# A selective state-space layer's first stage: the logarithm's table first, two casts on ScalarE, the first channels spread by 32-row products, and another order of the scan's steps

## The reference, cut to what matters

```
xn = _ln(x, ln1_g, ln1_b);  xm = _ln(xn, ln_g, ln_b)
xc = silu(conv(xm @ w1_w + w1_b))
delta = softplus(xc @ dt_w + dt_b)
Bt = xc @ Bp_w + Bp_b;  Ct = xc @ Cp_w + Cp_b
A = -exp(A_log)
for each position t:                       # h has 128 channels x 16 states
    h = exp(delta_t * A) * h + delta_t * Bt * xc_t
    y_t = sum over states of h * Ct
mo = ((y + D_p * xc) * silu(xm @ v1_w + v1_b)) @ w2_w + w2_b
x = mo + res;  ...feed-forward, residual, layernorm, next sublayer
```

## Time and profile before

| | |
|---|---|
| median of 3 runs | 486.89 us (486.88 to 487.8) |
| profiled execution | 487.24 us, of it 485.1 us span |
| busy of the span: PE, DVE, ACT, POOL | 87%, 63%, 43%, 30% |
| logarithm done on ScalarE | 24.4 us |
| first scan begins, last scan ends | 32.83 us, 63.62 us |

### The profile page before, as it was taken

One profiled execution on the slowest core, in us unless ns is written; L12 is line 12 of the kernel. 1 busy time (PEld: TensorE's weight loads), 2 busy tenths in 40 slices (PEclk: granted clock), 3 DMA queues, 4 the chain that ended last, 5 costly groups with the idle time before them and its releaser, 6 DMA issues.

```text
span 485.1 us, 7466 instructions
## 1 busy us (share of the span) xinstructions
PE 423.2 (87%) x2852; PEld 269.4 (56%) x2860; DVE 306.9 (63%) x712; ACT 206.8 (43%) x268; POOL 145.0 (30%) x138
## 2 busy tenths in 40 slices
PE   5867989999999999789999878698578999997984
PEld 5665645444555556556778355344434445556874
DVE  4789976676666665416213587953697777338754
ACT  1765623333333322153323388574154445546320
POOL 3226647877777774100302200000200000005111
PEclk9989999999999999999999887999998999999998
DMA  8611000000023110610440430000000000010000
GB/s 306 263 34 59 1 0 2 1 1 1 0 84 134 45 45 0 219 51 1 110 59 17 62 40 3 3 3 1 0 1 3 1 3 1 2 34 1 1 1 22
DMA packets 7791, 19.58 MB, mean 40 GB/s; under 512 B 1862, under 2 KB 3686, under 8 KB 7238
## 3 DMA queue, kind: packets, MB, share of 16 engines
q1 hardware_dynamic: 7756, 19.10, 13.5%
HBM read 17.26 MB, written 1.15 MB: 38 GB/s over the span
## 4 chain that ended last, share of the span: by engine, by line
PE 60%; DVE 21%; ACT 5%; issue 5%; POOL 5%; SPq 2%; DMA 1%; DVEq 0%; POOLq 0%
PE ps L1373 58%; DVE ps L1170 3%; DVE mx_a L1174 2%; POOL big L588 2%; SPq L445 1%; ACT big L768 1%; DVE big L983 1%; DVE ps L978 1%; POOL rstd L521 1%; PE ps L1385 1%; POOL big L595 1%; PE ps L1753 1%; DMA ident<-in_ident 1%; DVE big L1332 1%; DVE attn_w L917 1%
## 5 line engine op out<-in xcount | busy, mean ns | idle before, releaser
L1373 PE MATMUL ps<-big,late 128*32 128x256 f32 (+4 forms) x792 | 99.8, 383 | 11.8 <-DVE mid L909 4.5
L1373 PEld LDWEIGHTS ps<-big,late 128*32 128x32 f32 (+3 forms) x800 | 38.9, 117 | 52.0 <-issue 22.0
L794 ACT ACTIVATE big<-ps 128x1024 f32<-128x1024 f32 x48 | 48.9, 1023 | 40.3 <-PE ps L1373 39.8
L1373 PE MATMUL ps<-late,big 128*128 128x128 f32 (+1 forms) x448 | 64.1, 275 | 1.6 <-DVE mx_x L1170 1.3
L519 POOL TENSOR_SCALAR vareps<-meanvar 128x4 f32<-128x4 f32 (+2 forms) x11 | 2.6, 232 | 197.4 <-DVE meanvar L886 193.7
L732 ACT ACTIVATE big<-ps 128x1024 f32<-128x1024 f32 x32 | 32.8, 1024 | 65.3 <-PE ps L1373 58.9
L1373 PEld LDWEIGHTS ps<-late,big 128*128 128x128 f32 (+1 forms) x448 | 44.7, 152 | 25.2 <-issue 21.0
L588 POOL TENSOR_TENSOR big<-big 128x512 f32<-128x512 f32 x32 | 41.0, 1283 | 28.2 <-DVE big L1055 28.2
L1170 DVE CUSTOM_DVE_ANT_0 ps<-ps,big 128x512 f32<-128x512 f32 x64 | 42.6, 717 | 10.0 <-PE ps L1373 6.9
L1055 DVE TENSOR_SCALAR big<-big 128x1024 f32<-128x1024 f32 x32 | 27.6, 864 | 33.3 <-ACT big L732 33.3
L1373 PE MATMUL ps<-ident 128*128 128x128 f32 x232 | 30.3, 293 | 5.7 <-DMA ident<-in_ident 5.7
(11 more groups left out here) (255 smaller groups left out, 691.8 us busy)
## 6 DMA issues: line engine op xcount, KB each, us to landing
attn_w<-in_w_x SPq DMA_DIRECT2D x1, 2560.0 KB, 13.1
big<-parts_kx SPq DMA_DIRECT2D x18, 128.0 KB
late<-in_w_up SPq DMA_DIRECT2D x1, 2048.0 KB, 8.9
late<-in_w_dn SPq DMA_DIRECT2D x4, 512.0 KB, 3.9
attn_w<-in_w_up SPq DMA_DIRECT2D x1, 1024.0 KB, 5.9
attn_w<-in_w_dn SPq DMA_DIRECT2D x1, 1024.0 KB, 7.9
parts_kx<-ctx_r SPq DMA_DIRECT2D x1, 768.0 KB, 3.3
rowv<-in_rowv SPq DMA_DIRECT2D x1, 576.0 KB, 4.1
```

Source lines behind the costliest of these rows:

```text
L794: nc.scalar.activation(ex1[:, n % 3, :].rearrange("p (r n) -> p r n", r=2), ps[:, 2 * (n % 2):2 * (n % 2) + 2, :], ACT.Exp, scale=scale).t ...
L1373: return nc.tensor.matmul(o, lhsT, rhs, start=start, stop=stop, skip_group_check=shared)
```

## The change

- `nc.scalar.activation(act_table, ..., ACT.Ln, scale=-1.0)` stands behind xc's Silu, ahead of the exponentials; the one-element Exp call ahead of the loop is gone.
- delta's first and second bf16 part are made by ScalarE, the second behind `Cn`; the third part is made by VectorE instead of GpSimd. delta * xc is computed ahead of delta's remainder.
- q = 0 is not stacked: its six copies are gone. Its steps take three 32-row products per kind, straight from `dparts`, accumulating in the bank, each waiting for its own part.
- `ORDER` takes (0, 2), (1, 2) as steps 4 and 5, so q = 2 and 3 begin at step 6; the sums are called at steps 9, 11 and 14, with `SLOT` for the slots of `hC`.
- The 18 transfers are issued in the order of `QUADS`; the first eight hold the six of q = 1 and two of delta for q = 2 and 3.
- `values0(0, 0)` is no longer called at step 0; step 1 calls both `values0(0, 0)` and `values0(0, 1)`.

```diff
+        ORDER = ([(0, 0), (0, 1), (1, 0), (1, 1), (0, 2), (1, 2), (2, 0), (3, 0), (2, 1), (3, 1),
+                  (2, 2), (3, 2)] + [(q, 3) for q in range(4)])
+        SUMMED = ((0, 2, 6, 7), (1, 3, 8, 9), (4, 5, 10, 11), (12, 13, 14, 15))
+        SLOT = (0, 1, 2, 3, 4, 5, 6, 7, 0, 2, 6, 7, 1, 3, 0, 2)
+        QUADS = ([(0, 0, 1), (0, 0, 2), (0, 1, 1), (1, 0, 1), (0, 0, 3), (0, 2, 1), (1, 1, 1), (1, 2, 1)]
+                 + [(0, i, q) for q in (2, 3) for i in (1, 2)]
+                 + [(1, i, q) for q in (2, 3) for i in range(PARTS)])
...
-            pool.wait_ge(S["delta_parts"], 2)
-            nc.gpsimd.tensor_tensor(dparts[:, 0, 2, :], dtmp[:, 0, :], dparts[:, 0, 1, :], ALU.subtract
-                                    ).then_inc(S["delta_parts"], 1)
...
             nc.scalar.activation(xc[:], cv[:, 0, :], ACT.Silu).then_inc(S["xc_done"], 1)
+            nc.scalar.activation(act_table[:], neghalf[:, 0:1], ACT.Ln, scale=-1.0)
...
+            act.wait_ge(S["delta_done"], 1)
+            nc.scalar.activation(dparts[:, 0, 0, :], dl[:, 0, :], ACT.Copy).then_inc(S["delta_parts"], 1)
             nc.scalar.activation(Cn[:], ps[:, 5, :], ACT.Identity, bias=v("Cp_b")
                                  ).then_inc(S["BC_done"], 1)
+            act.wait_ge(S["delta_rest"], 1)
+            nc.scalar.activation(dparts[:, 0, 1, :], dtmp[:, 0, :], ACT.Copy
+                                 ).then_inc(S["delta_parts"], 1)
...
-            set_table(ACT.Exp)
-            act.wait_ge(S["delta_parts"], PARTS)
-            for i in range(PARTS):
-                ins = nc.scalar.activation(quads[32 * i:32 * i + 32, 0, 0, :], dparts[0:32, 0, i, :],
-                                           ACT.Copy)
-            ins.then_inc(S["delta_quads"], 1)
...
+            nc.vector.scalar_tensor_tensor(dl[:, 0, :], cv[:, 1, :], 0.0, dtmp[:, 2, :],
+                                           ALU.max, ALU.add).then_inc(S["delta_done"], 1)
...
+            dve.wait_ge(S["delta_parts"], 2)
+            dve.wait_ge(S["delta_rest"], 1)
+            nc.vector.tensor_tensor(dparts[:, 0, 2, :], dtmp[:, 0, :], dparts[:, 0, 1, :], ALU.subtract
+                                    ).then_inc(S["delta_parts"], 1)
...
-            for i in range(PARTS):
-                ins = nc.vector.tensor_copy(quads[32 * i:32 * i + 32, 1, 0, :], dparts[0:32, 1, i, :])
-            ins.then_inc(S["dx_quads"], 1)
...
+            def spread(kind, s, q, i):
+
+                bank = 2 * kind + s % 2
+                if q:
+                    return mm(ps[:, bank, :], sel_g[:, i, :], quads[:, kind, q, :])
+                for part in range(PARTS):
+                    pe.wait_ge(S[("delta_parts", "dx_parts")[kind]], part + 1)
+                    ins = mm(ps[:, bank, :], sel_g[0:32, i, :], dparts[0:32, kind, part, :],
+                             part == 0, part == PARTS - 1)
+                return ins
...
+                elif s == 6:
                     pe.wait_ge(S["late_quads"], 16 * 4 * PARTS)
...
-                if s in (7, 9, 14):
-                    y_of((7, 9, 14).index(s))
-                if s == 0:
+                if s in (9, 11, 14):
+                    y_of((9, 11, 14).index(s))
+                if s == 1:
 
                     pe.wait_ge(ld["x0"], 16)
                     pe.wait_ge(S["cxnT_done"], 2)
-                values0(s // 2, s % 2)
+                    values0(0, 0)
+                if s:
+                    values0(s // 2, s % 2)
```

More of the change, by code:

```diff
@@ L276, in program @@
             "dt_ps", "z_done", "BC_ps", "BC_done", "lg_done", "delta_parts", "dx_parts",
-            "delta_quads", "dx_quads", "second_quads", "late_quads",
+            "delta_done", "delta_rest", "second_quads", "late_quads",
             "spread_d", "spread_x", "dA_done", "dBx_done", "scan_done", "hC_done", "y_ps",
@@ L318, in own @@
             return link
-        ORDER = ([(0, 0), (0, 1), (1, 0), (1, 1), (2, 0), (3, 0), (2, 1), (3, 1)]
-                 + [(q, i) for i in (2, 3) for q in range(4)])
-        SUMMED = ((0, 2, 4, 5), (1, 3, 6, 7), (8, 9, 10, 11), (12, 13, 14, 15))
+        ORDER = ([(0, 0), (0, 1), (1, 0), (1, 1), (0, 2), (1, 2), (2, 0), (3, 0), (2, 1), (3, 1),
[5 more added lines that the diff above has]
+                 + [(1, i, q) for q in (2, 3) for i in range(PARTS)])
         KEYS = {"a": T, "x": CS}
@@ L438, in _ @@
             sp.dma_start(eb[:], a["eb"].partition_broadcast(P)).then_inc(ld["e1"], 16)
-            for q in (1, 2, 3):
-                for kind, parts in enumerate(("delta_parts", "dx_parts")):
-                    for i in range(PARTS):
[L444 to L447, removed]
+            for kind, i, q in QUADS:
+                sp.wait_ge(S["dx_parts" if kind else "delta_parts"], i + 1)
+                sp.dma_start(quads[32 * i:32 * i + 32, kind, q, :], dparts[32 * q:32 * q + 32, kind, i, :]
+                             ).then_inc(S["second_quads" if q == 1 else "late_quads"], 16)
             def spread_max(L):
@@ L541, in _ @@
                 if s >= 8:
-                    pool.wait_ge(S["y_ps"], 1 if s == 8 else 2)
-                nc.gpsimd.tensor_tensor(hC[:, s % 8, :], hs[:, s % 4, :], Cn[:],
+                    pool.wait_ge(S["y_ps"], 1 if s < 12 else 2)
+                nc.gpsimd.tensor_tensor(hC[:, SLOT[s], :], hs[:, s % 4, :], Cn[:],
                                         ALU.mult).then_inc(S["hC_done"], 1)
@@ L959, in _ @@
             dve.wait_ge(S["lg_done"], 1)
[L960 to L965, removed]
+            nc.vector.scalar_tensor_tensor(dl[:, 0, :], cv[:, 1, :], 0.0, dtmp[:, 2, :],
+                                           ALU.max, ALU.add).then_inc(S["delta_done"], 1)
+            dve.wait_ge(S["delta_done"], 1)
             dve.wait_ge(S["xc_done"], 1)
             link(nc.vector.tensor_tensor(dl[:, 1, :], dl[:, 0, :], xc[:], ALU.mult))
-            split(dl[:, 1, :], [dparts[:, 1, i, :] for i in range(3)], dtmp[:, 1, :], S["dx_parts"])
-            dve.wait_ge(S["dx_parts"], PARTS)
-            for i in range(PARTS):
-                ins = nc.vector.tensor_copy(quads[32 * i:32 * i + 32, 1, 0, :], dparts[0:32, 1, i, :])
-            ins.then_inc(S["dx_quads"], 1)
+            dve.wait_ge(S["delta_parts"], 1)
+            nc.vector.tensor_tensor(dtmp[:, 0, :], dl[:, 0, :], dparts[:, 0, 0, :], ALU.subtract
+                                    ).then_inc(S["delta_rest"], 1)
+            nc.vector.tensor_copy(dparts[:, 1, 0, :], dl[:, 1, :]).then_inc(S["dx_parts"], 1)
+            dve.wait_ge(S["dx_parts"], 1)
+            link(nc.vector.tensor_tensor(dtmp[:, 1, :], dl[:, 1, :], dparts[:, 1, 0, :], ALU.subtract))
+            dve.wait_ge(S["delta_parts"], 2)
+            dve.wait_ge(S["delta_rest"], 1)
+            nc.vector.tensor_tensor(dparts[:, 0, 2, :], dtmp[:, 0, :], dparts[:, 0, 1, :], ALU.subtract
+                                    ).then_inc(S["delta_parts"], 1)
+            nc.vector.tensor_copy(dparts[:, 1, 1, :], dtmp[:, 1, :]).then_inc(S["dx_parts"], 1)
+            dve.wait_ge(S["dx_parts"], 2)
+            nc.vector.tensor_tensor(dparts[:, 1, 2, :], dtmp[:, 1, :], dparts[:, 1, 1, :], ALU.subtract
+                                    ).then_inc(S["dx_parts"], 1)
             dve.wait_ge(S["BC_done"], 1)
@@ L1414, in _ @@
             pe.wait_ge(ld["sel"], 32)
-            pe.wait_ge(S["delta_parts"], PARTS)
             pe.wait_ge(S["gate_done"], 1)
@@ L1424, in y_of @@
                     q, i = ORDER[s]
-                    ins = mm(ps[32 * q:32 * q + 32, 4, :], sel_y[:, i, :], hC[:, s % 8, :],
+                    ins = mm(ps[32 * q:32 * q + 32, 4, :], sel_y[:, i, :], hC[:, SLOT[s], :],
                              i == 0, i == 3)
@@ L1448, in _ @@
                     pe.wait_ge(S["dA_done"], s - 1)
[L1449 to L1451 removed]
+                if s == 2:
                     pe.wait_ge(S["second_quads"], 16 * 2 * PARTS)
[L1453 removed]
+                elif s == 6:
                     pe.wait_ge(S["late_quads"], 16 * 4 * PARTS)
[L1455 to L1457 removed]
+                spread(0, s, q, i).then_inc(S["spread_d"], 1)
                 if s >= 2:
                     pe.wait_ge(S["scan_done"], s - 1)
[L1460 to L1464 removed]
+                spread(1, s, q, i).then_inc(S["spread_x"], 1)
+                if s in (9, 11, 14):
+                    y_of((9, 11, 14).index(s))
+                if s == 1:
                     pe.wait_ge(ld["x0"], 16)
                     pe.wait_ge(S["cxnT_done"], 2)
[L1468 removed]
+                    values0(0, 0)
+                if s:
+                    values0(s // 2, s % 2)
             pe.wait_ge(S["v0_done"], 2 * NPAIR)
```

## The result

The changed kernel takes 491.69 us (median of 6 runs, 489.44 to 493.07) against 487.35 (6 runs of before beside it, 486.88 to 488.24): ratio 1.0081, interval 1.0055 to 1.0107. It is slower; the forecast was 487.4, with 488.8 as the upper end. Repeated later beside 30 runs of before, it came out at 491.88, ratio 1.0055 (1.0033 to 1.0077). One execution of a later version, order_only, took 826.38 us and stands in no ratio.

What follows compares the result with a forecast made beforehand. The chain from softplus through transfers and scans bounds the kernel, VectorE pacing the loop. Terms -0.57, -0.49, +1.41, -0.75 and +0.86 gave +0.5: 487.4 us, range 486.9 to 487.9, over the cases 485.6 to 488.8.

Steps and rivals of the forecast that it cites:

- Ahead of the loop: From softplus to the first scan: added table load +1.50, shorter sequence behind it; first scan at 32.26 instead of 32.83, -0.57.
- Step 2: Eight value products partly at half clock, then the pair out at 36.7; scan 2 at 37.4 against 37.05, +0.35.
- I forecast the same fall and return: TensorE's clock ahead of scan 2 would halve at 32.0 and come back at 35.4, as in the kernel before.
- -1.05 at step 1: Scan 1 at 34.11 against 35.17 before, from -0.57 at the first scan and -0.49 more.
- the term that was put at +1.41: Step 2's share of the sum: loss from eight value products, partly at half clock, between steps 1 and 2.
- stays low longer: Rival, 22%: 32-row products delay the clock's return past about 36.1; scan 2 at 38.4 to 39.0, time 488.4 to 489.
- Step 4: No transfer left to wait for; scan 4 at 41.1 against 41.50, a term of -0.75.
- Step 12: Six products instead of two where TensorE is the limit, nothing hiding them: +0.86, scan 12 at 57.36.
- held-clock rival: Five short products in the gap keep the clock full; scan 2 at 35.96, -0.9, 486.0 us; chance 30%.
- So the effect on the time is the shift of the last scan: Nothing behind the loop absorbs a shift, so the total moves as the last scan does: 62.90 against 62.40.

Runs made afterwards that it cites:

- order_only: Kernel before with only the new order of steps, sums and transfers; stacks, casts and loads unchanged: ratio 0.9998 to before.
- no_ln: Changed kernel without the added one-element logarithm call: median 487.97 us, ratio 1.0001 to before.
- before_ln: Kernel before with only the added one-element logarithm call: ratio 1.0028 to before.
- stack12: Changed kernel with step 12 alone multiplied by two 96-row products, of parts stacked by six more transfers: 491.32 us, ratio 1.0043 to before.
- gap_full: Changed kernel with seven idle 128-row products between delta's three 32-row products: median 489.53 us, ratio 1.0024 to before.
- Combined: Changed kernel without the added call, step 12 stacked, three and two idle 128-row products, value products four and four: 487.10 us, ratio 0.9963 to before.
- gap_32: Changed kernel with seven idle products of only 32 rows between delta's three products: median 490.29 us, ratio 1.0064 to before.

## Why the prediction was wrong

- **Ahead of the loop: right.** Four loads; less the late start, the first scan is at 33.47 - 1.19 = 32.28 (forecast 32.26) and step 1's at 34.12 (34.11). The hit at step 1 is in part luck: in the repeat the clock fell some 0.9 us sooner after xc, and step 1 came 2.49 behind step 0. VectorE's undisturbed cast took 0.42, and six 32-row products 1.46, against 0.38 and five times 0.22, 1.48. The load cost 1.50 with its call. "ScalarE: Activation LUTs" of the Trainium skill, section "What ACT_TABLE_LOAD costs", adds a drain of some 1.4 us; taking the call out gave back 1.51 (no_ln), so this case shows none.
- **Step 2: the step that failed.** "I forecast the same fall and return" of the clock. In the profiled execution it fell where it was expected (33.2 - 1.2 = 32.0) and came back at 38.8 instead of 35.4. The eight value products ran at half throughout, so step 2's pair began at 38.03 - 1.19 = 36.84 instead of 36.13, and took half clock itself, 1.06. Scan 2 stands at 39.86 - 1.19 = 38.67 against 37.4: behind -1.05 at step 1, the term that was put at +1.41 is +2.67 (38.67 is 1.62 behind the earlier trace rows). This is the rival "stays low longer", which had 22% and gave 38.4 to 39.0 for scan 2. Its reason, the 32-row products in the stretch that should bring the clock back, is not shown: before_ln and order_only stay low as long with 96-row pairs. It was the length of before's one fall, taken over as a constant, that did not carry. Why it is 3.4 us in before and 6.8 in the others stays open.
- **Step 4.** The wait for the transfer went, as forecast (order_only). In the profiled execution 0.43 of it was lost again there, since TensorE was still catching up (2.28 from step 3 to step 4); in the repeat it was not.
- **Step 12: right in kind, 0.1 short.** +0.86 forecast; stack12 measures 0.96. The two rows, 1.46 and 0.60, give the 0.86.
- **The total.** The front lost 2.24 to 2.36 where +0.5 was forecast. With the 0.9 of the held-clock rival (gap_full: 44.34 - 43.47 = 0.87) it is the clock that decides between -0.9 and +2.3. "So the effect on the time is the shift of the last scan" failed as well: behind that scan it is some 1.5 us more in the first profile and 2.7 in the repeat, and the median, 491.69, lies past the long fall's 488.4 to 489 too. Of the 1.5, 1.4 is a low clock near 200 us, present in both profiles of the changed kernel (3.4 and 6.8 us long) and in neither of before; whether the change in the front brings it about is open, and with before's own spread it may come without the change too. Combined has it with a held clock in the front, gap_32 doesn't have it with a long fall.

## What to carry to other kernels

When a change puts waits between TensorE's products, price the stretch at either clock and ask which work would lie in it: here the same instructions, but for seven idle products, were worth -0.9 or +2.3 us in the front. Try full-height idle products in such a wait, no longer than the wait; three, 0.94 us, were enough here without the added call, and two more where TensorE had no wait put step 2 off by 0.57. A product of few rows keeps TensorE busy in the profile, but that is no sign that its clock will hold.

## What the runs showed of the hardware

With idle products that kept TensorE busy for about as long (3.30 and 3.12 of 3.3 us), the granted clock stayed at 2.4 GHz behind 128-row ones and fell to 1.2 GHz behind 32-row ones. A fall ahead of step 2 lasted 3.4 us in one kernel and 6.8 in seven others, and for the two kernels with a second profile it lasted as long again. Half clock does not reach VectorE: its scan stays at 1.22 us in all 14 profiles.
